# Second attention of a six-stage program: one unrolled plan, two heads per maxima job on 64-row tiles, triangle zeroed on GpSimd

## The reference

```
q = rope(x @ Wq.T), k = rope(x @ Wk.T), v = x @ Wv.T      # 16 heads of 16 features
scores = einsum("bhsd,bhtd->bhst", q, k) / sqrt(256)
scores = where(t > s, -inf, scores)
out = einsum("bhst,bhtd->bhsd", softmax(scores), v) @ Wo.T
```

## Time and profile before

| | |
|---|---|
| median of the runs | 2342.56 us |
| the profiled execution | 2343.61 us |
| its span, first to last instruction | 2341.8 us |
| mean granted clock of TensorE | 0.934 of 2.4 GHz |
| busy: PE, DVE, ACT, POOL | 87%, 72%, 43%, 42% |
| the attention heads | 1652.9 to 2285.7 us of the span |
| their first and last score | 1707.3 and 2281.6 us |

### The profile page before, as it was taken

The page is one execution under the profiler, slowest core; times in us unless marked ns, Lnnn a source line. Parts: engine busy times, 40 slices in busy tenths (PEclk is TensorE's granted clock), DMA queues, the critical chain, the costliest instruction groups (busy, mean ns, idle before and its releaser), DMA issues. The chain is left out here.

```text
span 2341.8 us, 36616 instructions
## 1 busy us (share of the span) xinstructions
PE 2037.0 (87%) x10632; PEld 1205.8 (51%) x10632; DVE 1676.4 (72%) x3188; ACT 1000.3 (43%) x2042; POOL 975.4 (42%) x865
## 2 busy tenths in 40 slices
PE   4757999999999999999999999567699998999996
PEld 3634555555555555555555554455454554554545
DVE  6667877878778778687787784775586785767825
ACT  1223343443434434434434434111167666666771
POOL 0023685795775856956957766013300000000000
PEclk8867999999999999999999999678799999999998
DMA  2200000000000000000000000110000000000001
GB/s 84 65 8 5 8 1 5 9 1 5 8 1 12 1 5 8 1 5 8 1 5 0 1 1 0 39 39 23 1 1 1 1 1 1 2 2 1 1 1 37
DMA packets 19790, 23.26 MB, mean 10 GB/s; under 512 B 4128, under 2 KB 17952, under 8 KB 19488
## 3 DMA queue, kind: packets, MB, share of 16 engines
q1 hardware_dynamic: 18416, 20.00, 2.8%
q10 hardware_dynamic: 1200, 1.31, 0.2%
HBM read 19.21 MB, written 2.10 MB: 9 GB/s over the span
## 5 line engine op out<-in xcount | busy, mean ns | idle before, releaser
L1100 ACT ACTIVATE lath_probs<-lath_shifted 128x512 f32<-128x512 f32 (+3 forms) x640 | 357.8, 565 | 683.3 <-DVE lath_shifted L1211 650.5
L1177 POOL TENSOR_TENSOR lath_summed<-lath_summed,lath_probs 128x512 f32<-128x512 f32 (+3 forms) x528 | 584.6, 1128 | 122.4 <-ACT lath_probs L1100 112.4
L1211 DVE TENSOR_TENSOR lath_shifted<-lath_score,lath_shift 128x512 f32<-128x512 f32 (+3 forms) x640 | 385.3, 607 | 147.8 <-PE lath_score L986 131.5
L1218 DVE TENSOR_REDUCE lath_maxima<-lath_max 128x1 f32<-128x512 f32 (+3 forms) x640 | 380.3, 605 | 132.4 <-PE lath_max L1007 84.8
L1623 DVE TENSOR_REDUCE atth_maxima<-atth_max 128x1 f32<-128x512 f32 (+3 forms) x640 | 355.1, 605 | 98.2 <-PE atth_max L1746 54.2
L1702 ACT ACTIVATE atth_probs<-atth_score 128x512 f32<-128x512 f32 (+3 forms) x640 | 313.6, 536 | 178.4 <-PE atth_score L1760 92.0
L994 PE MATMUL lath_out<-lath_probs,lat_latent 128*64 128x512 f32 (+3 forms) x1280 | 307.2, 559 | 0.0
L1007 PE MATMUL lath_max<-lat_key_hi,lath_query_hi 128*128 128x512 f32 (+3 forms) x640 | 266.0, 424 | 18.0 <-DVE lath_maxima L1218 16.5
L1746 PE MATMUL atth_max<-atth_key,atth_query 128*128 128x512 f32 (+3 forms) x640 | 267.3, 429 | 15.1 <-DVE atth_query L1595 6.2
L982 PE MATMUL lath_score<-lath_query_hi,lat_key_hi 128*128 128x512 f32 (+3 forms) x640 | 265.9, 415 | 4.0 <-DVE lath_shifted L1211 4.0
L1760 PE MATMUL atth_score<-atth_query,atth_key 128*128 128x512 f32 (+3 forms) x640 | 246.6, 407 | 14.0 <-ACT atth_probs L1702 11.6
(11 more groups left out here) (341 smaller groups left out, 2839.3 us busy)
## 6 DMA issues: line engine op xcount, KB each, us to landing
ffn_a_w<-in_L_ffn_W SPq DMA_DIRECT2D x2, 1024.0 KB, 11.7
lat_raw_out<-in_L_attn_w_out SPq DMA_DIRECT2D x8, 256.0 KB, 2.7
lat_rope<-in_c_rope_feature SPq DMA_DIRECT2D x1, 2048.0 KB, 10.8
ffn_b_w<-in_L_ffn_W SPq DMA_DIRECT2D x2, 1024.0 KB, 7.6
mix_a_factors<-in_L_ffn_factors SPq DMA_DIRECT2D x8, 256.0 KB, 4.1
out<-x SPq DMA_DIRECT2D x4, 512.0 KB, 2.9
lat_raw_q<-in_L_attn_w_q_b SPq DMA_DIRECT2D x8, 192.0 KB, 2.4
x<-in_L_attn_x ACTq DMA_DIRECT2D x2, 512.0 KB, 7.0
```

What stands on the lines that cost most here:

```text
L1100: nc.scalar.activation(probs[:, prob_slot(j, kt), h, q0:CH], shifted[:, 2 * (kt % 2) + h, q0:CH], ACT.Exp, scale=SCALE0).then_inc(s["exp_d ...
L1177: last = nc.gpsimd.tensor_tensor(summed[:, j % 2, h, q0:CH], so_far, probs[:, prob_slot(j, kt), h, q0:CH], ALU.add)
L1211: nc.vector.tensor_tensor(shifted[:, 2 * (kt % 2) + h, q0:CH], score_bank[score_place(j, kt, h) % 3][:, q0:CH], shift[:, j % 2, h, q0:CH], ...
L1218: nc.vector.reduce_max(maxima[:, h, i, kc:kc + 1], max_bank[(i * (nj + 1) + kc) % 2][:, 0:width], AX.X).then_inc(s["maxima_taken"], 1)
```

## The change

`attention_heads` is written anew, with a new plan; nothing else changes.

- `attention_plan` replaces the tables and the loop. It walks all 16 (group, chunk) pairs once, with a time for each event, and all is unrolled with constant waits. The last group takes its chunks as 3, 2, 1, 0. The maxima of a chunk may run ahead of its scores by up to four query tiles (`QUERY_TILES`). Only the maxima of chunk 0 stand before the first score.
- The zero halves are gone: `atth_query` holds two heads on 128 partitions, and score and maxima matmuls take 64 rows of the array each, rows 0 to 63 for even heads and 64 to 127 for odd ones. `atth_key` and `v_one` are doubled, for even and odd groups.
- The side bank and the three maxima banks become two slots of two banks, `atth_slot`. Every maxima job and every turn takes a slot in turn; job r waits until job r-2 is read out. A "whole" job is two matmuls (two heads, each its own bank) and one reduction over 2 x 512 columns. The diagonal squares of a pair are one "triangle" job: two 512-wide bfloat16 mask matmuls, eight 128-wide matmuls, one reduction. What lies below the diagonal inside a chunk is the jobs "odd" and "even". This makes 288 jobs and 320 reductions.
- Keys, queries and shifted queries are turned for all four heads at once (eight transposes), and read out in one instruction of 1024 columns: keys by VectorE, queries by ScalarE.
- Scores get no mask. GpSimd sets the triangle of `atth_probs` to zero with `affine_select`, four heads at once, one for each of the 64 diagonal steps; the values wait for it.
- GpSimd takes three copies per chunk from ScalarE (the second parts of the slots, and the values).

```diff
-MAXIMA_STEPS = [(-11.1, -8.55), (-6.9, -0.4), (-0.5, 9.7), (9.4, 22.8)]
+QUERY_TILES = 4
+STEP_TIME = 2.45
+CHUNKS = [(g, j) for g in range(NG - 1) for j in range(NCH)] + [(NG - 1, j) for j in reversed(range(NCH))]
+def maxima_jobs(j):
+    for pair in range(2):
+        yield pair, "triangle", 0, ((0, CH),)
+        yield pair, "odd", 0, ((1, P), (3, 3 * P))
+        yield pair, "even", 0, ((2, 2 * P),)
+        for i in range(TPC):
+            for kc in range(j):
+                yield pair, "whole", kc, ((i, CH),)
+def attention_plan():
...
+        begin = max(maxima_end, ended[n - QUERY_TILES] + 3.0 if n >= QUERY_TILES else 0.0)
+        at = begin
+        for k, job in enumerate(maxima_jobs(j)):
+            jobs.append((at, 0.0, ("maxima", n, k, *job)))
+            at += 0.18 * len(job[3]) + sum(width for _, width in job[3]) / 480
+        maxima_end = at
+        jobs.append((at + 1.6, 1.2, ("shifted", n)))
+        step_end = max(step_end, at + 4.5)
+        for kt in range(key_tiles(j)):
+            length = STEP_TIME * (0.2 + 0.8 * (CH - max(kt - TPC * j, 0) * P) / CH)
+            others += [(step_end + 0.25 * h * length, ("scores", n, kt, h, len(step_ends))) for h in range(GROUP)]
...
# TensorE
-                            wait(pe, s["maxima_taken"], m - 2 if maxima_place(j, h, i, kc) else m)
-                            mm = nc.tensor.matmul(bank[:, 0:width], query[:, j % NCH, h, i * P:(i + 1) * P],
-                                                  key[:, h // 2, kc * CH:kc * CH + width], start=True, stop=(kc < nj))
+                    if kind in ("maxima", "keys", "queries", "shifted", "finish") and a[0] >= 2:
+                        wait_taken(pe, a[0] - 2)
...
+                                for h in range(2):
+                                    last = nc.tensor.matmul(slot[r % 2][:, h, begin:begin + width],
+                                                            query[rows_of(h), n % QUERY_TILES, pair, i * P:(i + 1) * P],
+                                                            key[g % 2][rows_of(h), pair, first:first + width], start=True, stop=True)
...
+                        wait(pe, s["exp_done"], u - 2)
+                        nc.tensor.matmul(score_bank[u % 3][:, q0:CH], key[g % 2][rows_of(h), h // 2, kt * P:(kt + 1) * P],
+                                         query[rows_of(h), n % QUERY_TILES, h // 2, q0:CH], start=True, stop=True).then_inc(s["scores_done"], 1)
...
+                        if step in masks_before:
+                            pe.wait_ge(s["masked"], masks_before[step] + 1)
# VectorE
+                                nc.vector.reduce_max(maxima[:, n % 2, heads, i, at], slot[r % 2][:, :, begin:begin + width], AX.X)\
# GpSimd
+                    elif kind == "mask":
+                        pool.wait_ge(s["exp_done"], GROUP * (step + 1))
+                        own = probs[:, step % 4, :, q0:q0 + P]
+                        nc.gpsimd.affine_select(own, own, [[0, GROUP], [1, P]], ALU.is_ge, 0.0, base=0, channel_multiplier=-1)\
+                          .then_inc(s["masked"], 1)
```

More of the change, by code:

```diff
@@ L1507, in attention_heads @@
+    counts, read = {}, {True: 0, False: 0}
+    for e in plan:
+        if e[0] in reads:
+            scalar = e[0].startswith(TAKEN_BY_SCALAR)
+            read[scalar] += len(e[7]) if e[0] == "maxima" else reads[e[0]]
+            counts[e[2]] = read[scalar]
+    group_end = {g: max(e[3] for e in plan if e[0] == "values" and CHUNKS[e[1]][0] == g) for g in range(NG)}
     with ExitStack() as ctx:
```

550 lines of the change are left out of this document (236 added, 314 removed).

## The result

The changed kernel takes 2366.10 us, median of four runs (2353.57 to 2367.42), against 2344.04 for the kernel before on the same chip: ratio 1.0085, interval 1.0052 to 1.0118. It is slower by some 20 us; 157 us less were forecast. The profiled execution, the shortest of the four, took 2353.57 us with a span of 2351.9, and its mean granted clock fell from 0.934 to 0.906.

What follows compares the result with a forecast made beforehand. It took TensorE's list to set the pace in the heads' long part. Terms of 10 + 92 + 322 + 48 + 4 = 476 us replaced the heads' 632.7, 157 less, giving 2187 us; range 2120 to 2285.

Steps and rivals of the forecast that it cites:

- Start: From the start of the heads to the first reduction: 10 us, against 13.8 before, as the query memsets go.
- Maxima of the first four chunks: First reduction until chunk 3's 16 steps start: VectorE sets the pace, TensorE has room; 92 us.
- The other 136 steps: Steps after the first four chunks' maxima: 97 full ones at 2.59 us, 39 narrower ones 71 us; together 322 us.
- turns: Transposes of keys and queries, turns back and triangle jobs on TensorE: 77 us, 29 hidden in full steps, 48 left.
- the shadow of the fourth score: In each step the fourth score waits 1.17 us for the first exponential; both maxima jobs fit in that wait.
- term 4: Turns and triangle jobs in the remaining 12 chunks: 77 us of TensorE time, 29 hidden in steps' spare, 48 left.
- If TensorE idles at each turn: Sign named beforehand that the prediction is wrong: TensorE standing idle at transposes of keys or queries; given no size.
- End: Last drain, turn and division at the end of the heads: 4 us, as in the kernel before.
- Dear changes of form: Rival: switching into or out of 64-row tiles costs more; from 0.5 us per change slower, 2360 or so; chance 0.07.
- No overlap: Rival: the two 64-row matmuls of a pair do not run at the same time; say 2260 us; chance 0.17.
- late selects: Rival: GpSimd's triangle mask takes 3 us each and holds up the diagonal's values; about 2240 us; chance 0.06.
- VectorE's pace: Rival: VectorE, not TensorE, sets the pace throughout the heads; 2111 to 2140, say 2125 us; chance 0.18.

Runs made afterwards that it cites:

- The full-height run: Changed kernel with score, maxima and triangle matmuls over 128 rows instead of 64, exponential scale 1e-4 of its own; 2367.40 us, ratio 1.0107 to the kernel before.

## Why the prediction was wrong

Of 647.7 us against 476, by its own terms:

- **Start** (10 us): 11.4 (1648.06 to 1659.50). Right.
- **Maxima of the first four chunks** (92 us): 131.7, until chunk 3's first score at 1791.24. Wrong by 40. VectorE was to be the pace, with TensorE having room; but VectorE is busy for 94.5 of these us and TensorE for 106.7, and VectorE waits for jobs. At the end of chunk 2 no new step begins for 20.8 us, while nine jobs, four turns and the turn back of an output go through the two buffers one after the other. 50 us of this term are at 1.2 GHz, by the estimate 15 to 20 us of loss; the rest is put down to stops, of which this stretch is the longest.
- **The other 136 steps** (322) **and turns** (48): 370 forecast, 498 measured, 1791.24 to the last score at 2289.3. The step itself was right, 2.61 with overlap and 3.04 without (forecast 2.59 and 3.07), and so was the shadow of the fourth score. The step's price came out although the matmuls do not pair as assumed: the two of a job start together in only half of the whole jobs. Two things failed. First, the full-speed price was taken for all steps: 143 of the 498 us are at 1.2 GHz, an estimated 51 us of loss. The prediction priced the changes of form and the drain, but took the clock of before, 0.98, as given. The run of the kernel before on 64 rows shows that the new form itself lowers it (0.66). Second, term 4 counted TensorE's own time of a turn (1.17 us) and set it against the spare in steps; but a turn also holds TensorE's list until another engine has reached the copy on its list and done it. Idle stretches after 1791 are 67 us. "If TensorE idles at each turn" was among the signs that would make it wrong, and it was not priced. The full-height run shows that these stops stand at a clock of 0.96 too: 220 us for the same 32 steps.
- **End** (4): 6.4, from the last score to the end (4.1 before). Off by 2.

Start, ramp and the rest are off by 1, 40 and 128, with the end's 2 together the 172 us; by the estimate some 70 of them are the clock, and about 100 are stops with what they drag along. The split is an estimate; that both are there is measured. This account is of the profiled execution; the other three runs took 12 to 14 us longer at a mean clock of 0.896 to 0.899 instead of 0.906, so there the clock's part is larger still.

**The rivals.** Dear changes of form, the rival on the slower side, did not happen: they cost 0.1 to 0.2 us in and 0.2 back, close to the 0.35 taken for both. The prediction's count of changes in the kernel before, 236, is too low: it has the loop over groups 1 and 2 once, and the trace has 316, against 478 in the changed kernel. It came out slower by another mechanism, to which the prediction gave no chance. "No overlap" is refuted by the trace, late selects too (0.64 us, where 1.3 were assumed). VectorE's pace is refuted: VectorE waits.

**What each part is worth.** The triangle on GpSimd gives 15 us, shown alone. The rest of the rewrite at full height (changed, 128 rows, against before with the triangle on GpSimd) costs 1.8%: 1.0107 against 0.9930, with 32 us more idle and 31 us more at 1.2 GHz. So the ring of two buffers, the plan and the moved copies together cost more than fewer instructions on VectorE bring; they were not tried one by one. The 64 rows on top give 0.43 us a step and take it back by the clock: 1.0085 against 1.0107, the intervals overlap.

**What stays open.** The clock fell in runs that moved events without changing any matmul (0.80 with turns or values moved, 0.86 unmoved), so the time at 1.2 GHz depends on order as well as on the 64-row form; by which rule is not shown, nor whether it is the height or the running side by side that counts. Whether a bank of its own for turns would remove the stops was not tried; the stage holds eight (four for the slots, three for scores, one for outputs), as before.

## What to carry to other kernels

Before a change of tile form, ask for the clock as well as for the columns: here 64-row matmuls saved 0.43 us a step by overlap and lost it again by the clock. A transfer through a shared buffer costs, beside its length, the time until its reader comes to it on the other engine's list; read the lists of both. Try parts alone: the small one, masks off the pacing engine onto an idle one, gave 15 us, and nothing else in the change is shown to give any.

## What was not expected of the hardware

- TensorE 97% busy with matmuls over 64 rows had a granted clock of 0.66 for 857 us, and the same instructions over 128 rows, half of them zeros, 0.98 (94% busy, 533 us).
- A change between full height and 64-row tiles costs 0.1 to 0.2 us in and 0.2 back (medians 0.36 and 0.43 against 0.235 from start to start), and none was seen between the two row halves.
- GpSimd's select on 128 x 512 float32 takes 0.64 us, half of its arithmetic on as many columns.
